# Row gathers of a mixture-of-experts layer: one float32 one-hot product, or two float32r products of rows split in two

## The reference, cut to what matters

```python
expert_weights, token_indices = jax.lax.top_k(expert_probs, cap)      # cap = 32
expert_weights = expert_weights / (expert_weights.sum(-1, keepdims=True) + 1e-09)
expert_inputs = jax.vmap(lambda h, i: h[i])(hidden_states, token_indices)
gate = jax.nn.silu(jnp.einsum('becd,edf->becf', expert_inputs, w1))
value = jnp.einsum('becd,edf->becf', expert_inputs, w2)
expert_out = jnp.einsum('becf,efd->becd', gate * value, w3)
```

## Time and profile before

| | |
|---|---|
| timed executions | 513.41, 515.21, 516.83 us (median 515.21) |
| span of the profiled execution | 513.1 us |
| time of the profiled execution itself | not among the three times; the span is 0.3 us under the lowest |
| TensorE busy | 487.3 us (95%) |
| VectorE busy | 354.2 us (69%) |
| ScalarE busy | 288.2 us (56%) |
| GpSimd busy | 234.4 us (46%) |
| mean granted TensorE clock | 0.989 |
| products that gather (L1609) | 16 in the program, 32 in the trace, 16.9 us busy |

### The profile page before, as it was taken

How to read it: one execution, slowest core, us unless ns; L and a number is a source line. 1 busy time by engine, 2 the same in 40 slices (tenths; PEclk the granted TensorE clock), 3 DMA queues, 4 the chain that set the end, 5 groups by cost and what they waited for, 6 DMA issues and landing times.

```text
span 513.1 us, 13570 instructions
## 1 busy us (share of the span) xinstructions
PE 487.3 (95%) x5109; PEld 378.7 (74%) x5113; DVE 354.2 (69%) x1000; ACT 288.2 (56%) x984; POOL 234.4 (46%) x331
## 2 busy tenths in 40 slices
PE   4799999998999999999999999899999999999996
PEld 3466766656668778887787777788757897799995
DVE  5888989766786678566786665757866588535553
ACT  3366566463586776666867657665664444413332
POOL 4845545035365544575444755324231980090440
PEclk9699999999999999999999999999999999999999
DMA  8900000000001100111000000022202100000001
GB/s 229 234 3 4 3 3 3 3 1 8 4 1 32 34 20 16 34 33 34 3 2 2 4 3 3 1 66 64 64 0 71 56 0 1 1 22 24 1 2 42
DMA packets 21872, 14.48 MB, mean 28 GB/s; under 512 B 5928, under 2 KB 21136, under 8 KB 21808
## 3 DMA queue, kind: packets, MB, share of 16 engines
q1 hardware_dynamic: 20704, 13.31, 9.6%
q10 hardware_dynamic: 1104, 0.30, 0.3%
HBM read 12.30 MB, written 1.05 MB: 26 GB/s over the span
## 4 chain that ended last, share of the span: by engine, by line
PE 79%; DVE 12%; ACT 3%; issue 2%; DMA 1%; POOL 1%; ACTq 0%; DVEq 0%; POOLq 0%
PE bank L1792 9%; PE bank L1721 6%; PE bank L1551 5%; PE bank L1558 5%; PE bank L1801 5%; PE bank L1538 5%; PE bank L1510 5%; PE bank L1374 5%; PE bank L1463 5%; PE bank L1521 4%; PE bank L1530 4%; PE bank L1808 3%; PE bank L1609 3%; PE bank L1359 3%; ACT work L1150 2%
## 5 line engine op out<-in xcount | busy, mean ns | idle before, releaser
L1150 ACT ACTIVATE work<-bank,negmax 128x124 f32<-128x124 f32 x256 | 90.0, 387 | 52.2 <-DVE ipa_s L775 52.0
L498 POOL TENSOR_TENSOR work<-work,rsum 128x496 f32<-128x496 f32 x64 | 64.1, 1012 | 120.2 <-DVE rsum L789 120.2
L533 POOL TENSOR_SCALAR work<-work,slot 128x128 f32<-128x128 f32 x64 | 49.7, 792 | 48.3 <-DVE slot L864 29.4
L1150 ACT ACTIVATION_READ_ACCUMULATOR work<-bank,negmax 128x1 f32 x256 | 58.9, 230 | 0.0
L1792 PE MATMUL bank<-work 128*128 128x256 f32 x224 | 53.4, 381 | 0.0
L1014 DVE SCALAR_TENSOR_TENSOR work<-work,bank 128x256 f32<-128x256 f32 x64 | 26.9, 421 | 33.0 <-ACT work L1302 32.8
L1302 ACT ACTIVATE work<-bank 128x256 f32<-128x256 f32 x64 | 24.5, 383 | 40.6 <-PE bank L1792 29.1
L481 POOL TENSOR_TENSOR work<-work 128x512 f32<-128x512 f32 (+2 forms) x48 | 39.2, 817 | 12.1 <-DVE work L745 9.6
L306 DVE TENSOR_TENSOR x_all<-bank,x_all 128x128 f32<-128x128 f32 x16 | 4.7, 292 | 57.4 <-PE bank L1721 55.4
L1792 PEld LDWEIGHTS bank<-work 128*128 128x128 f32 x224 | 40.3, 190 | 4.7 <-DVE work L1017 0.2
L773 DVE TENSOR_REDUCE negmax<-bank 128x4 f32<-128x496 f32 x64 | 42.5, 664 | 0.0
(11 more groups left out here) (197 smaller groups left out, 1101.1 us busy)
## 6 DMA issues: line engine op xcount, KB each, us to landing
work<-in_L_ffn_w_dram SPq DMA_DIRECT2D x42, 128.0 KB, 2.3
x_all<-in_x_dram SPq DMA_DIRECT2D x4, 256.0 KB, 5.8
out_dram<-x_all SPq DMA_DIRECT2D x4, 256.0 KB, 2.6
ctx_all<-in_ctx_dram SPq DMA_DIRECT2D x4, 192.0 KB, 6.0
ctx_all<-in_L_ffn_w_dram SPq DMA_DIRECT2D x6, 128.0 KB, 2.3
work<-in_L_xattn_Wq_dram SPq DMA_DIRECT2D x1, 512.0 KB, 6.5
work<-in_L_xattn_Wo_dram SPq DMA_DIRECT2D x1, 512.0 KB, 8.2
work<-in_L_ffn_We_dram SPq DMA_DIRECT2D x1, 512.0 KB, 5.7
```

The source lines that it names most:

```text
L498: pool.tensor_tensor(part, part, rsum1[:, b % 2, CH * n:CH * n + CH].unsqueeze(2).broadcast_to((128, CH, ORG)), ALU.mult).then_inc(Z.norm, 1)
L533: ins = pool.tensor_scalar(ohw_of(e)[:, k, :], count[:, :], slot[:, h, 0, k, e % E1:e % E1 + 1], slot[:, h, 1, k, e % E1:e % E1 + 1], ALU. ...
L1150: ins = act.activation(p1[:, b % 2, n, c, 0:ORG], blocks(bank[n])[:, c, 0:ORG], ACT.Exp, bias=negmax1[:, b % 2, h:h + 1], accum_out=sums1[ ...
```

## The change

The normalized rows are split on VectorE, four batches at a time: `xn_hi` is the row written as float32r, `xn_lo` is what is left, written as float32r. The gather becomes two products that accumulate in the same bank, first of `xn_hi`, then of `xn_lo`, both with a one-hot matrix that is written as float32r. The split of batches 0 to 3 is called in round 11, of 4 to 7 in round 12, of 8 to 11 at expert 2 and of 12 to 15 at expert 3. The three new tensors are permanent; ten tensors of the first layer, permanent before, move into the arena over tensors used later. The number of one-hot comparisons, of token broadcasts and of copies out of PSUM stays.

```diff
+F32R = mybir.dt.float32r
...
-        k0T = sb("k0T", [128, 4, 128])
-        q0T = sb("q0T", [128, 2, 128])
...
+        work.again(p1T_at, p1T_at + H * S + 8 * 128)
+        k0T = work.take([128, 4, 128])
+        own_col = work.take([128, CH, 128])
...
-        oh = work.take([128, 2, E1, CAP])
...
+        xn_hi = sb("xn_hi", [128, HB, D], F32R)
+        xn_lo = sb("xn_lo", [128, HB, D], F32R)
+        oh = sb("oh", [128, 2, E1, CAP], F32R)
...
-        G = named(sem, "g", "told oh got xg")
+        G = named(sem, "g", "hi lo told oh got xg")
...
+            def split(g):
+
+                part = slice(4 * (g % 2), 4 * (g % 2) + 4)
+                whole, hi, lo = xn_half[g // 2][:, part, :], xn_hi[:, part, :], xn_lo[:, part, :]
+                dve.wait_ge(R.xn, 4 * g + 4)
+                after(dve, G.got, 4 * (g - 1))
+                dve.tensor_copy(hi, whole).then_inc(G.hi, 1)
+                dve.wait_ge(G.hi, g + 1)
+                dve.tensor_tensor(lo, whole, hi.bitcast(F32), ALU.subtract).then_inc(G.lo, 1)
...
                 if b in (10, 11):
                     normalize(xn_half[0], 4 * (b - 10), 4 * (b - 9), rstd_at["half", 0], R.xn)
+                if b in (11, 12):
+                    split(b - 11)
...
                 if e in (2, 3):
                     hidden(e)
+                    split(e)
...
                 if b >= HB:
                     after(pe, G.xg, b - 1)
-                pe.matmul(bank[got_in(b)][:, :], xn_half[b // HB][:, b % HB, :], oh[:, b % 2, :, :].rearrange("p e s -> p (e s)"),
-                          start=True, stop=True).then_inc(G.got, 1)
+                pe.wait_ge(G.lo, b // 4 + 1)
+                picked = oh[:, b % 2, :, :].rearrange("p e s -> p (e s)")
+                pe.matmul(bank[got_in(b)][:, :], xn_hi[:, b % HB, :], picked, start=True, stop=False)
+                pe.matmul(bank[got_in(b)][:, :], xn_lo[:, b % HB, :], picked, start=False, stop=True).then_inc(G.got, 1)
```

More of the change, by code:

```diff
@@ L135, in build_program @@
         first_row = sb("first_row", [128, CH])
-        own_col = sb("own_col", [128, CH, 128])
-        pick0 = sb("pick0", [128, CH, 128], BF16)
         bq0 = sb("bq0", [128, 1])
@@ L175, in build_program @@
         p1 = work.take([128, 2, CH, CH, S])
+        p1T_at = work.at
         p1T = work.take([128, H, S])
@@ L196, in build_program @@
         tanhs4 = work.take([128, 4, 128])
+        work.again(p1T_at, p1T_at + H * S + 8 * 128)
+        k0T = work.take([128, 4, 128])
+        own_col = work.take([128, CH, 128])
+        q0T = work.take([128, 2, 128])
+        rsum0 = work.take([128, 2, 128])
+        o0T = work.take([128, 2, 128])
+        pick0 = work.take([128, CH, 128], BF16)
+        q0_bf = work.take([128, 3, 128], BF16)
+        xn_in = work.take([128, 3, D])
+        negmax0 = work.take([128, 2, 128], BF16)
+        negmax0T = work.take([128, 2, 128], BF16)
         work.again(0, attn0_end)
```

## The result

The changed kernel takes **512.29 us** (median of 8 runs, 510.93 to 515.36) against 515.60 for the kernel before, timed beside it (8 runs, 513.41 to 516.83): ratio 0.9935, 95% interval 0.9909 to 0.9961. The forecast was 512.0, within 1%.

A forecast was written before the change was run, and what follows sets the result against it. TensorE, busy 95% of the span, was taken as the bound. Terms -3.44 - 1.4 + 1.1 + 0.1 + 0.5 = -3.1, rounded to -3.2, from 515.2 gave 512.0 us; range 509.2 to 517.0.

The forecast's parts named there:

- float32r streams once: Each gather: two float32r products of 0.22 us replace one float32 product of 0.86, saving 0.43 us a gather.
- Rivals 2 and 3: Gathers: a float32r product takes 0.43 us, total 516.9 us, chance 0.12; or 0.86 us, total 529 us, chance 0.06.
- Stage B gives all, nothing is absorbed: Second gathering stage (426 to 445 us), TensorE full: all 8 gathers on the path, 3.44 us off.
- Three gathers pay in stage A: First gathering stage (368 to 393 us): three of 8 gathers pay 0.43 us each, plus 0.1; 1.4 us off.
- Rival 4: First gathering stage pays in full and the splits at experts 2 and 3 are free: -5.8, 509.4 us; chance 0.09.
- Split 0 in full, split 1 hidden: VectorE's cast and subtraction ahead of round 12 cost +1.1 us in full; one round later, mostly covered, +0.1.
- Splits 2 and 3, +0.5: At experts 2 and 3: split of 1.9 us with GpSimd waits, 0.85 then 1.1 free; +0.5 us, ends 0 and 2.1.
- rival 1: At experts 2 and 3, GpSimd holds VectorE for whole instructions: split 2.7, cost 2.1 not 0.5; 513.6 us, chance 0.13.

## Why the prediction was right

- **float32r streams once: right, the entry a little longer than forecast.** The short end of the bounds was taken, 0.22 an entry; 0.23 was measured. The saving is 0.40 a gather and not 0.43 (0.86 - 0.46), and a broadcast among float32r entries takes 0.23 in place of 0.22. 8 x 0.40 - 6 x 0.01 = 3.1, where stage B gave 3.06 in place of 3.44. Rivals 2 and 3 would have shown entries of 0.43, or gathers of 1.72.
- **Stage B gives all, nothing is absorbed: right.** The chain is TensorE alone, what follows is equal to 0.01 us, and with half the entries left out the stage gave another 1.66.
- **Three gathers pay in stage A: right.** -1.28 for -1.4. The waits of 0.75, about 0.7 and 0.31 stand at the places named or next to them. Round 15 lost 0.40 (gather 3), round 16 0.88 (gathers 5 and 6, and 0.08 each for 4 and 7). Rival 4, all eight, falls.
- **Split 0 in full, split 1 hidden: right.** +1.07 and +0.08 for +1.1 and +0.1, shown by the splits alone, by the doubling and by the move.
- **Splits 2 and 3, +0.5: wrong, the step was mis-sized.** The hold by GpSimd had been put at 0.4 us for each instruction, half of a GpSimd instruction; it is 0.13 for the subtraction and 0 to 0.05 for the cast. A split is 1.24 in place of 1.9, less than the 0.85 and 1.1 that were free, and 1.4 of cover were left over. The hold was carried over from L835, which had met another GpSimd instruction than the tables. The cover was put too small as well: doubled, a split is 2.55, nearly the 2.7 of rival 1, and the two cost 1.21, not its 2.1. Rival 1 falls with it. The rule of the Trainium skill cited there (page "SBUF — State Buffer", section "Who interferes with whom") holds in kind: a subtraction with two operands in the on-chip memory is slowed by a GpSimd instruction that reads there, 0.82 against 0.69. Its block for the whole instruction agrees with L835's 1.05, but no split was held for a whole table instruction, 0.79.
- Two errors of opposite sign, +0.5 too much for the splits and 0.4 too much from stage B, with 0.1 from stage A, cancelled in the sum. The forecast of -3.2 was met by -3.23 in the trace, a little better than its terms deserved.

## What to carry to other kernels

A shorter product is worth what its stage says: the full stage gave 3.06 for eight gathers, the stage with holes 1.28 for eight, and the holes grew by the rest. Preparation for it belonged here into the engine's longest wait and not merely somewhere ahead of its use: the same two VectorE instructions cost 1.07 us in front of a round's first maxima and nothing some 10 us later in the round, inside a wait of 5 us. Where start-up varies by 4 us and the change is worth 3, compare stretches from a marker that both programs share; they repeat to 0.1 us.

## What the runs showed of the hardware

- A float32r product with 128 rows and 512 columns is one weight load (0.19 us) and one entry, 0.23 us on the chain; the float32 product is two entries and 0.86. With bfloat16 operands it is 0.10 and 0.22. Two float32r products thus cost just over half of a float32 one.
- VectorE writes 128x512 float32r at the price of the nearest rows: cast 0.41 to 0.42, subtraction 0.69, the same when the result is bfloat16. The cast L593 of the earlier trace rows took 428 ns.
- A bfloat16 product of 512 columns among float32r ones takes 0.23 and among bfloat16 ones 0.22, with loads of 0.10 for itself and 0.19 to 0.20 for its successor in both. Why is open.
- VectorE's L835 lasted to the end of a GpSimd TENSOR_TENSOR of 1.01 us, 1.05 in place of 0.29; beside the tables' TENSOR_SCALAR of 0.79 us L835 and the splits lost at most 0.17. Two of the table instructions took 0.95 and 1.05 beside the splits of after, so the hold goes both ways.
